# Three block ends carried into the next block of a one-core decoder kernel

## Time and profile before

| what | value |
|---|---|
| median of 3 runs | 1213.46 us (1210.11 to 1218.25) |
| profiled execution, its own time | 1208.43 us |
| its span, first to last instruction | 1206.6 us |
| mean granted PE clock | 0.958 |
| busy: PE, DVE, ACT, POOL | 89%, 70%, 48%, 22% |

### The profile page before, as it was taken

The page is one execution under the profiler, slowest core; times in us unless marked ns, Lnnn a source line. Parts: engine busy times, 40 slices in busy tenths (PEclk is TensorE's granted clock), DMA queues, the critical chain, the costliest instruction groups (busy, mean ns, idle before and its releaser), DMA issues. The chain is left out here.

```text
span 1206.6 us, 24266 instructions
## 1 busy us (share of the span) xinstructions
PE 1073.4 (89%) x8935; PEld 665.8 (55%) x8950; DVE 848.9 (70%) x2010; ACT 581.6 (48%) x1582; POOL 263.7 (22%) x331
## 2 busy tenths in 40 slices
PE   9798979999889998798998968689999998789955
PEld 5466656777533333344555548477777776344422
DVE  3699676999757788479984897734477878833326
ACT  2445334554246667464552427167777775322212
POOL 5201000111201111305333110400000000157742
PEclk9899787999889999999999999999999999989987
DMA  6733333000022322070000002085000000759566
GB/s 197 104 91 110 99 83 102 2 2 2 1 79 79 111 79 80 17 137 1 2 1 1 2 1 68 22 268 169 19 19 19 23 23 27 210 178 243 86 139 249
DMA packets 83040, 94.82 MB, mean 79 GB/s; under 512 B 19808, under 2 KB 66854, under 8 KB 82662
## 3 DMA queue, kind: packets, MB, share of 16 engines
q1 hardware_dynamic: 73484, 79.72, 23.1%
q0 software_dynamic: 6496, 9.57, 4.3%
q10 hardware_dynamic: 2944, 3.98, 0.9%
HBM read 68.65 MB, written 21.97 MB: 75 GB/s over the span
## 5 line engine op out<-in xcount | busy, mean ns | idle before, releaser
L401 DVE TENSOR_REDUCE gqa_x_slots<-gqa_scores 128x8 f32<-128x1024 f32 x64 | 78.4, 1226 | 31.4 <-PE gqa_scores L288 22.4
L1572 DVE TENSOR_REDUCE mla_neg_max<-mla_scores 128x8 f32<-128x1024 f32 x32 | 39.2, 1225 | 77.1 <-PE mla_scores L1437 51.5
L1519 ACT ACTIVATE mla_probs<-mla_scores,mla_neg_max 128x128 f32<-128x128 f32 x256 | 90.3, 390 | 0.0
L358 ACT ACTIVATE gqa_expT<-gqa_scoresT 128x1024 f32<-128x1024 f32 x64 | 65.6, 1025 | 50.1 <-PE gqa_scoresT L309 50.1
L309 PE MATMUL gqa_scoresT<-gqa_x_slotsT,gqa_keys 32*128 32x512 f32 x256 | 73.9, 649 | 10.8 <-issue 5.0
L288 PE MATMUL gqa_scores<-gqa_keys_bd,xT 32*128 32x512 f32 x256 | 73.5, 670 | 2.7 <-DVE gqa_x_slots L401 1.4
L1427 PE MATMUL mla_q_ps<-xT,mla_merged_home 128*128 128x128 f32 x512 | 64.3, 280 | 1.6 <-PEq L63 1.6
L1427 PEld LDWEIGHTS mla_q_ps<-xT,mla_merged_home 128*128 128x128 f32 x512 | 61.2, 196 | 2.0 <-issue 1.8
L1460 PE MATMUL mla_out_ps<-mla_merged_home,mla_attT 128*128 128x256 f32 x256 | 60.7, 380 | 0.7 <-ACT mla_attT L1532 0.7
L2645 PEld LDWEIGHTS ttt_z_ps<-ttt_g_pairs,ttt_masked 128*64 128x64 f32 x1024 | 53.4, 141 | 12.2 <-issue 11.4
L1519 ACT ACTIVATION_READ_ACCUMULATOR mla_probs<-mla_scores,mla_neg_max 128x1 f32 x256 | 58.6, 229 | 0.0
(11 more groups left out here) (466 smaller groups left out, 2639.5 us busy)
## 6 DMA issues: line engine op xcount, KB each, us to landing
moe_w_gu<-in_moe_w_gu SPq DMA_DIRECT2D x24, 384.0 KB, 5.7
gqa_keys_bd<-in_gqa_keys_bd SPq DMA_DIRECT2D x16, 512.0 KB, 3.4
moe_w_dn<-in_moe_w_down SPq DMA_DIRECT2D x24, 192.0 KB, 6.6
moe_sums<-moe_zeros SPq DMA_DIRECT2D x2, 2176.0 KB, 12.0
ttt_by_token<-ttt_g_pairs SPq DMA_DIRECT2D x4, 576.0 KB, 4.6
ttt_lanes<-ttt_by_token SPq DMA_DIRECT2D x16, 144.0 KB, 5.9
xT<-in_x_feat SPq DMA_DIRECT2D x4, 512.0 KB, 7.8
x_tok<-in_mla_woT SPq DMA_DIRECT2D x8, 256.0 KB, 3.3
```

Source lines behind the costliest of these rows:

```text
L358: nc.scalar.activation(expT[:, k % 2, 2 * u:2 * u + 2, :], scoresT[:], ACT.Exp, scale=HD ** -0.5).then_inc(exp_ready, 1)
L401: nc.vector.tensor_reduce(x_slots[:, b % 2, :, c * NJ + 2 * half:c * NJ + 2 * half + 2, HD].rearrange("p g j -> p j g"), scores[:, of].rea ...
L1519: ins = nc.scalar.activation(probs[:, k % NB, e, i, :], scores[:, k % 2, e, i, :], ACT.Exp, bias=neg_max[:, k % 2, e, i:i + 1], accum_out= ...
```

## The change

Work at three block ends is issued in the next block instead. Its semaphores are made in a list `across` that is not given back, and cross-attention, feed-forward and batch-axis attention share one PSUM tensor `banks` of all eight banks, so that a bank can outlive its block.

- **Cross-attention** now runs steps -1 to 32. `CrossLast` holds `weigh`, `turn_back`, `copy_weighted`, `divide`, `add` and the norm. Feed-forward issues what is left: PE turn_back(30) after tile 0, weigh(31) and the transposes of sequence 14 after tile 1, turn_back(31) after tile 2, the transposes of sequence 15 after tile 4; DVE divide(30) and the normalisation of 14 ahead of tile 0's product, divide(31) and add(15) in tile 2, the normalisation of 15 in tile 3. POOL's cast of the down weights comes one norm earlier.
- **Feed-forward** ends with `down(15)` and norm 14. `FfnLast` holds sequence 15's scale, add and norm: batch-axis attention issues them first on DVE and POOL (POOL ahead of its memsets), the transposes on PE after the first four projections, the copy on ACT after keeping those four.
- **Batch-axis attention** ends when the last strip is kept; its attended values get an SBUF home of their own. SP issues the loads of the merged weights and goes on without waiting. `AttendedOut` issues the 16 rows in latent attention: five rows ahead (`AHEAD`), the other eleven among units 0 to 2 (`SHARED`), up to four in a unit. Both norms share one transposing bank, so each row's transposes wait for the copy of the row before.
- The homes of five expert pairs lie in the attended values; SP loads these only when the last row's product is read.
- All `keep_busy` calls at these three places go.

```diff
 # cross-attention
-        STEPS = range(-1, NU + 5)
+        STEPS = range(-1, NU + 1)
...
-                if k == NU + 3:
-                    keep_busy(nc, scoresT[:, 0, :], ...)
 # feed-forward, PE
             for n in range(END):
                 if n < TILES:
                     up(n)
+                if n == 0:
+                    cross.turn_back(pe, cross.NU - 2)
+                if n == 1:
+                    cross.weigh(pe, cross.NU - 1)
+                    cross.norm.tensor(pe, B - 2)
+                if n == 2:
+                    cross.turn_back(pe, cross.NU - 1)
+                if n == 4:
+                    cross.norm.tensor(pe, B - 1)
...
-                    if sequence_at(n - 3) == B - 1:
-                        keep_busy(nc, gate_ps[:, 0], ..., 11)
 # feed-forward, DVE
+                if n == 0:
+                    cross.divide(dve, order, cross.NU - 2)
+                    cross.norm.vector_end(dve, B - 2)
                 if n < TILES:
                     fuse(n)
...
+                if n == 2:
+                    cross.divide(dve, order, cross.NU - 1)
+                    cross.add(dve, order, B - 1)
+                if n == 3:
+                    cross.norm.vector_end(dve, B - 1)
 # batch-axis attention
             project(qk(0), qk(1))
+            ffn.norm.tensor(pe, B - 1)
...
-            for n in range(L):
-                out(n)
-                if n >= 2:
-                    norms[n % 2].tensor(pe, n // 2 - 1)
 # latent attention, PE
+            for n in range(AHEAD - 1):
+                row_out(n)
+            pe.wait_ge(latent.merged_loaded, 16 * len(latent.merged_loads))
             project(0)
-            keep_busy(nc, attT_ps[:], ..., 1)
+            row_out(AHEAD - 1)
             for k in range(LAST):
                 if in_range(k):
                     score(k)
+                for n in rows_in(k, 0):
+                    row_out(n)
...
                 if in_range(k + 1):
                     project(k + 1)
+                for n in rows_in(k, 1):
+                    row_out(n)
+                if k == SHARED - 1:
+                    rows.turn(pe, B - 2)
+                    rows.turn(pe, B - 1)
+                    turn(k - TURN_LAG, 0)
 # latent attention, DVE
+            for n in range(AHEAD):
+                row_norm(n)
+            for k in range(SHARED):
+                keep_max(k)
+                for n in rows_in(k, 0):
+                    row_norm(n)
+                if in_range(k - 1):
+                    divide(k - 1)
+                for n in rows_in(k, 1):
+                    row_norm(n)
+            rows.end(dve, B - 1)
+            for rows_norm in rows.norms:
+                dve.wait_ge(rows_norm.kept, B // 2)
```

More of the change, by code:

```diff
@@ L262, in _ @@
                 fill(b)
-            for b in range(B):
+            for b in range(B - 2):
                 norm.gpsimd(pool, b)
@@ L422, in _ @@
                 if 0 <= k - 3 < NU:
-                    divide(k - 3)
+                    last.divide(dve, order, k - 3)
                 if k + 1 < NU:
@@ L500, in gated_ffn_int8 @@
         h_rest_ready, x_rest_ready = sem("h_rest_ready"), sem("x_rest_ready")
-        down_ready, y_ready, chain = sem("down_ready"), sem("y_ready"), sem("chain")
-        norm = Norm(nc, ctx, "ff_n", keep, normT, addend=batch_axis.b_out[:])
-        next_loads = latent.open(ctx, keep, io) + batch_axis.loads
+        down_ready, y_ready, norm, chain = last.down_ready, last.y_ready, last.norm, sem("chain")
+        next_loads = latent.open(ctx, keep, io, cross.start) + batch_axis.loads
         block = ctx.enter_context(nc.Block())
@@ L608, in _ @@
                     hidden_third(n - 1)
-                if b is not None:
-                    scale_and_add(b)
+                if b == 0:
+                    dve.wait_ge(cross.norm.kept, B)
+                if b is not None and b < B - 1:
+                    last.scale_and_add(dve, order, b, down[b % 2])
                 if n < TILES:
                     hidden_rest(n)
+                if n == 2:
[3 more added lines that the diff above has]
+                    cross.norm.vector_end(dve, B - 1)
                 if group_to_split(n):
@@ L878, in batch_axis_attention @@
         lanes_loaded = [sem(f"lanes_loaded{n}") for n in range(EB)]
-        out_ready, chain, merged = sem("out_ready"), sem("chain"), sem("merged")
-        norms = [Norm(nc, ctx, f"ba_n{k}", keep, turned_ps[:, k, 0:D], place=lambda n, k=k: 2 * n + k, count=L // 2) for k in range(2)]
+        chain = sem("chain")
         QUARTERS = T * L // 512
@@ L1100, in _ @@
                 keep_attended(s)
-            for n in range(L):
-                norms[n % 2].scalar(act, n // 2)
-            for norm in norms:
-                norm.done(act)
+            act.wait_ge(att_kept, STRIPS)
         @block.vector
@@ L1384, in latent_cross_attention @@
         norm = Norm(nc, ctx, "mla_n", keep, normT)
+        rows = AttendedOut(nc, ctx, keep, inputs, attended, [out_ps, attT_ps[:, 0:D]], turned[:, 0:D])
+        AHEAD, SHARED = 5, 3
+        rows_in = lambda k, part: [n for n in range(AHEAD + 4 * k + 2 * part, AHEAD + 4 * k + 2 * part + 2) if k < SHARED and n < B]
         TURN_LAG, WEIGH_LAG = 2, 3
@@ L1412, in _ @@
             nc.gpsimd.memset(moe.zeros[:], 0.0).then_inc(moe.zero_set, 1)
+            for n in range(B):
+                rows.gpsimd(pool, n)
             for b in range(B):
```

367 lines of the change are left out of this document (231 added, 136 removed).

## The result

Over 18 runs each the median went from 1212.18 to 1198.09 us; the ratio is 0.9898, its 95% interval 0.9878 to 0.9919, which in us is 12.4 (9.8 to 14.8). The three terms of the forecast summed to 13.2, and its median was 1200.3. The profiled execution of the changed kernel took 1195.27 us (span 1193.3).

The account below looks back on a forecast made before the run. PE was taken to bound feed-forward and latent attention, with no engine full at the block ends. Terms -4.2 - 2.8 - 6.2 = -13.2 us took 1213.46 to 1200.3; range 1192.5 to 1209.

Parts of the forecast that it names:

- first end: Cross-attention into feed-forward: tail -8.29, carried PE work +2.66, stall in tile 4 +1.4; sum -4.2 us, bounds -5.6 and -3.0.
- second end: Feed-forward into batch-axis attention: tail -3.11, first score sums 0.3 later; sum -2.8 us, bounds -3.1 and -1.5.
- third end: Batch-axis rows into latent attention: rows and units share time, score(3) at 796.0 against 802.18; -6.2 us.
- from score(3) on the queues of all engines are as before: Latent attention behind the shared stage: nothing changes from score(3) on, so the -6.2 us there carries through.
- the clock falling below 1.00 in the shared stage: Latent attention's units shared with the rows: PE's granted clock below 1.00 would show the prediction wrong.
- Rival 3: PE at its lower clock level throughout the shared stage: score(3) 16.4 us late, total 1222.9; chance 0.04.
- Rival 1: Carried work held up more, by DVE and POOL meeting, feed-forward's stall and engine changes: 5.2 us less gain, 1205.5; chance 0.26.
- Rival 2: DVE's waits in the shared stage don't come: 4.4 us more gain, 1195.9; chance 0.14.
- Rival 4: Borders wait for something other than ACT's last copy and the tails stay: only -3 us, 1210.5; chance 0.06.

Follow-up runs that it names:

- the reordering: Changed kernel with the next row's output products issued ahead of each project(k+1), the previous row's transposes behind it: 1198.67 us, ratio 0.9880.
- The fillers: Changed kernel with six extra 256-column matmuls on PE in the thin end of the shared stage: 1194.54 us, ratio 0.9861.
- score(3) alone: Changed kernel with score(3) issued ahead of the last two rows' transposes, its keep_max ahead of the last normalisation: 1200.65 us, ratio 0.9891.
- the three edits together: Changed kernel with next row's output products ahead of each project(k+1), thin end filled with later work, sequence 15's transposes in tile 5: 1190.24 and 1191.53 us.

## Why the forecast came out

**The sum.** Forecast -4.2, -2.8 and -6.2, in all -13.2. From the table: first end -8.64 + 3.76 = -4.9; second end -3.1 + 0.2 = -2.9; third end, to score(4), -6.4 + 1.8 = -4.6. In all -12.4. That this is the ratio's figure to the tenth is chance, as the interval of that is 9.8 to 14.8, and the profiles of other runs move the terms: the first is 2.4 to 3.3 where the clock fell in cross-attention's last steps, the third 7.3 against the profile with the rows put back. The total was right within its range, in part by luck: an error of 0.7 one way in the first term and of 1.6 the other way in the third.

**First end.** The tail of 8.29 is 8.3. The carried work on PE plus stall was put at 2.66 + 1.4 = 4.06 and is 3.8: the stall, in the place that was named, is 1.09. What was left out is the border, assumed to stay at 1.1: it is 0.80 before the first weight load, where it was 1.13. With the end undone the first matmul comes 1.16 after ACT's last copy, as in the kernel before. Which instruction at the block's end holds the other engines that long was not tested.

**Second end.** Gain and price as forecast. The 11 filler matmuls that went with it were not missed.

**Third end, to score(3).** Forecast -6.2, measured -6.4, with two errors of about a microsecond that cancel. Two waits at 1.61 and 1.57 were put at 1.8, those of 0.4 at rows 11 and 15 didn't come, the last power was 1.06 for 1.1; DVE was through 38.6 after the block's first instruction, where I had 40.0. The chain behind it took 3.7 instead of 2.7, because the two turns ran at the low clock. That the waits come from project's place in PE's queue is shown by the reordering.

**Third end, behind score(3).** This is the step that failed: "from score(3) on the queues of all engines are as before". The queues are, the clock isn't. From score(4) on the stage is as it was: to the experts' first matmul it is 221.0 and 220.9 us before, 220.8 and 221.0 changed. So the error of the third term lies between the last rows and score(4). The prediction had named the clock falling below 1.00 in the shared stage as a sign that it is wrong, and by that sign it was, though the total held. Rival 3 had looked at the stage as a whole, found it denser than the one before, and set 0.04 on all of it being low; the low stretch that came is where the stage is thinnest, at its end, and it costs 1.6 to 2.0 between score(3) and score(4) and some 0.7 in the turns. The fillers, which add work and nothing else, give 2.6 back. The same list of PE's instructions that I walked through to find DVE's waits would have shown PE with little to do behind the last row's products: busy 0.9 of 4 us. The Trainium skill, page "TensorE: Matmul & The Clock Gate", Part 1, says that idleness puts the engine at 1.2 GHz and work brings it back; the windows here agree (0.56 behind the thin stretch, 1.00 from 791.4 on). The forecast used that rule only for the stage's average.

**Rival 1 and the shared port.** Divide and power did meet. POOL's timeline in the changed kernel, at the first divide, beside what DVE did:

```profile
765.23 1.27 DVE L1711 TENSOR_TENSOR mla_probs<-mla_probs,mla_rsum 128x1024 f32<-128x1024 f32 x1
765.38 1.53 POOL L171 TENSOR_TENSOR ba_n_rstd<-ba_n_var_eps,neg_half 128x1 f32<-128x1 f32 x1
```

The power takes 1.53 where 14 others in the stage take 0.55; at the second divide, at 774.79, it is 1.53 again. DVE's own product is 1.27, against 1.23. So POOL was held twice by 1.0, and the end didn't move: DVE needs that power only behind the next row's begin, and shows no wait there. The Trainium skill, page "SBUF — State Buffer", section "Who interferes with whom", says that the shared ports are an exclusive lock and that the order of issue decides who blocks. The trace agrees: the divide began 0.15 ahead of the power, and it was the power that took longer. What the block costs, the queue behind it decides. **Rival 2** was wrong for rows 4 and 7. **Rival 4** was wrong: all three tails are gone.

**What stays open.** The experts' stage took 176.1 and 176.7 us in the two profiles of the kernel before; in the twelve of kernels with the new homes of the weights it took 176.9 to 184.1, four of them under 178, with a median of 180.1. So both profiles of before lie below all twelve, and the profiles by themselves point to a shift. In neither kernel does PE wait there for a load of expert weights, which is how new homes could cost time. Some of the waiting there is DVE's for scatters to land, 15.0 and 24.4 us in the two profiles of before, 24.0 and 29.0 in those of the changed kernel, so that alone tells nothing. A shift of 3 us or more would make the sum of the terms 9.4 or less, outside the interval that the runs give; a smaller one is neither shown nor excluded.

## What to carry to other kernels

When work is carried over a border, walk the queue of the engine with the clock through the place where the last carried item and the first own items meet: what was a dense stage in the mean may have a thin end, and a few idle microseconds there slow what comes next. Fill it, best with pieces of work that come later anyway (-4.4 us here, against -2.6 for filler matmuls), and see to it that the piece does not leave a new gap behind it, as score(3) alone did. If two engines hand rows to each other, a long step of the one belongs behind the next row's product, not between a row's transposes and it; how much that gives depends on what follows directly behind the step.

## What was not expected of the hardware

Single executions of one kernel differ by some 20 us, and the profiles show where up to half of it arises: up to cross-attention's first reduction it took from 328.0 to 337.9 us, with the same instructions. The windows of that stretch, of the kernel before, of its repeat, and of the three edits together:

```profile
0.00:335.00 335.00, 305.33 (x3374) 210.04 (x3374) 254.62 (x707) 137.73 (x398) 54.79 (x89) 0.92 0.28 72
```

```profile
0.00:330.00 330.00, 301.17 (x3374) 207.06 (x3374) 254.06 (x708) 137.74 (x398) 55.22 (x90) 0.94 0.29 74
```

```profile
0.00:328.00 328.00, 298.40 (x3374) 205.69 (x3374) 253.86 (x707) 137.66 (x398) 54.83 (x90) 0.95 0.29 73
```

The same 3374 matmul records, and a granted clock of 0.92, 0.94 and 0.95: the shorter the stretch, the higher the clock. Feed-forward has the same in small: with its end as changed, the first down product to the batch-axis start took 116.9 us in seven profiles, 118.4 and 118.6 in two, and 119.9 and 120.0 in two. In one of the last, that with fillers, a second stretch at a lower clock stood where the changed kernel had none. These are the windows around it, with fillers and then the same stretch of the changed kernel, which runs it 3 us earlier:

```profile
628.00:637.00 9.00, 6.49 (x48) 5.04 (x46) 5.69 (x16) 1.88 (x4) 1.68 (x3) 0.81 0.01 2
```

```profile
625.00:634.00 9.00, 6.45 (x56) 5.12 (x53) 6.29 (x18) 1.88 (x4) 2.15 (x4) 1.00 0.00 0
```

PE is about equally busy, 6.49 and 6.45 of 9 us, and once the clock fell and once it didn't. A stretch of that density can go either way, so that two profiles with a full clock there, as those of the kernel before behind its tail, are no promise.
